# Idle matmuls from a VectorE-filled tile, and another order of the first groups, in a graph layer with a layer norm

## The reference, cut to what matters

```python
msg = jax.nn.relu(node_feat[src] + edge_attr)                      # a gather of 25000 rows
agg = jax.ops.segment_sum(msg, dst, num_segments=node_feat.shape[0])
h = node_feat + agg
h = jax.nn.relu(h @ W1 + b1) @ W2 + b2                             # 128 -> 256 -> 128
out = _layernorm(x + jax.nn.relu(h), axis=-1)
```

## Time and profile before

| | |
|---|---|
| median of three runs | 459.33 us (459.14 to 460.5) |
| profiled execution | 459.34 us |
| its span | 457.7 us |
| TensorE (PE) busy | 450.5 us, 98% |
| VectorE (DVE) busy | 433.3 us, 95% |
| ScalarE (ACT) busy | 394.6 us, 86% |
| GpSimd (POOL) busy | 370.1 us, 81% |
| mean granted TensorE clock | 0.997 |

### The profile page before, as it was taken

One profiled execution on the slowest core, in us unless ns is written; L12 is line 12 of the kernel. 1 busy time (PEld: TensorE's weight loads), 2 busy tenths in 40 slices (PEclk: granted clock), 3 DMA queues, 4 the chain that ended last, 5 costly groups with the idle time before them and its releaser, 6 DMA issues.

```text
span 457.7 us, 10675 instructions
## 1 busy us (share of the span) xinstructions
PE 450.5 (98%) x3046; PEld 380.4 (83%) x3046; DVE 433.3 (95%) x1759; ACT 394.6 (86%) x930; POOL 370.1 (81%) x403
## 2 busy tenths in 40 slices
PE   8999999999999999999999999999999999999995
PEld 7888888888888888888888888888888888888884
DVE  6899999999999999999999999999999999999996
ACT  3599888888888889988888888888888888888886
POOL 7778888888888878778888888888888888888842
PEclk9999999999999999999999999999999999999998
DMA  5576666666566666666666666666666666666632
GB/s 135 164 234 199 201 187 201 194 195 203 181 197 202 181 199 202 185 192 200 197 205 190 201 190 195 194 194 200 198 195 197 186 199 202 185 203 191 196 126 90
DMA packets 83870, 86.82 MB, mean 190 GB/s; under 512 B 12023, under 2 KB 79508, under 8 KB 83812
## 3 DMA queue, kind: packets, MB, share of 16 engines
q1 hardware_dynamic: 75044, 68.77, 48.2%
q0 software_dynamic: 8496, 17.38, 14.1%
q10 hardware_dynamic: 272, 0.00, 0.0%
HBM read 60.51 MB, written 25.60 MB: 188 GB/s over the span
## 4 chain that ended last, share of the span: by engine, by line
PE 98%; DVE 1%; ACT 0%; POOL 0%; issue 0%; DVEq 0%; POOLq 0%
PE h_ps L1052 38%; PE h1T_ps L1044 36%; PE hT_ps L965 11%; PE hT_ps L960 9%; PE h1T_ps L464 1%; PE prep_ps L451 0%; DVE stats L696 0%; PE hT_ps L936 0%; PE hT_ps L953 0%; DVE z L689 0%; PE h1T_ps L1032 0%; ACT std L851 0%; PE hT_ps L454 0%; ACT h1T L846 0%; PE h1T_ps L1025 0%
## 5 line engine op out<-in xcount | busy, mean ns | idle before, releaser
L135 POOL DMA_INDIRECT x_src<-in_x_dram,src_of x254 | 270.3, 1064 | 65.5 <-issue 59.8
L1052 PE MATMUL h_ps<-w_sb,h1T 128*128 128x128 f32 x1564 | 197.5, 276 | 0.0
L1044 PE MATMUL h1T_ps<-hT,w_sb 128*128 128x384 f32 x520 | 188.5, 485 | 0.0
L1052 PEld LDWEIGHTS h_ps<-w_sb,h1T 128*128 128x128 f32 x1564 | 185.2, 192 | 0.0
L846 ACT ACTIVATE h1T<-h1T_ps,b_sb 128x384 f32<-128x384 f32 (+1 forms) x262 | 151.5, 579 | 35.4 <-PE h1T_ps L1044 27.1
L1044 PEld LDWEIGHTS h1T_ps<-hT,w_sb 128*128 128x128 f32 x520 | 88.7, 191 | 34.2
L865 ACT ACTIVATE y<-z,shift,rstd 128x128 f32<-128x128 f32 x263 | 114.6, 483 | 1.1 <-DVE shift L716 0.2
L596 POOL TENSOR_SCALAR y<-z,rstd,shift 128x128 f32<-128x128 f32 x123 | 87.7, 713 | 13.5 <-DVE shift L716 9.0
L965 PE MATMUL hT_ps<-sel,msg_hi 128*128 128x216 f32 x250 | 94.8, 447 | 0.0
L696 DVE BATCH_NORM_STATS2 stats<-z 128x6 f32<-128x128 f32 x391 | 88.6, 282 | 0.1
L960 PE MATMUL hT_ps<-ident,x_sb 128*128 128x128 f32 x375 | 87.5, 272 | 0.0
(11 more groups left out here) (139 smaller groups left out, 187.9 us busy)
## 6 DMA issues: line engine op xcount, KB each, us to landing
x_sb<-in_x_dram SPq DMA_DIRECT2D x130, 192.0 KB, 2.4
out_dram<-y SPq DMA_DIRECT2D x130, 192.0 KB, 2.4
pre_msg<-in_edge_attr_dram SPq DMA_DIRECT2D x130, 128.0 KB, 2.8
x_src<-in_x_dram,src_of POOLq DMA_INDIRECT x254, 3.0
w_sb<-in_w_dram SPq DMA_DIRECT2D x2, 128.0 KB, 2.6
dst_rows<-in_dst_dram SPq DMA_DIRECT2D x1, 97.7 KB
x_src<-in_x_dram,first_pairs POOLq DMA_INDIRECT x6, 2.8
b_sb<-in_b_dram SPq DMA_DIRECT2D x1, 64.0 KB, 3.3
```

The lines of the kernel that those rows point to most:

```text
L135: nc.gpsimd.indirect_dma_start(out=c["x_src"][:, g % EB, k, :], out_offset=None, in_=x, in_offset=bass.IndirectOffsetOnAxis(ap=index, axis ...
L1044: nc.tensor.matmul(h1T_ps[h][:, 0:n, 0:p], w1_sb[:, h * 128:(h + 1) * 128], hT[:, 0:n, 0:p], start=True, stop=True).then_inc(h1_summed, 1)
L1052: last = nc.tensor.matmul(h2_ps[g % 2][0:p, t, :], h1T[:, h, t, 0:p], w2_sb[:, h, :], start=(h == 0 and t == 0 and not biased(g, c)), stop ...
```

## The change

The idle matmuls read a new tile `filler`, which VectorE fills with ones as its second instruction, and wait for that; there are nine of them instead of seven. The wait for the identity moves behind the two first search products. Group 0's six transposes (three into `hT_ps`, three into `rest_ps`) and the third search product stand together ahead of the wait for group 0's messages. `hidden_part` moves ahead of `turn_starts` and `sum_whole`. The product of group 0 by W2 is split and moves up: its first half stands ahead of the last product of group 1, its second half behind it, and both ahead of `turn_windows`. VectorE counts the first row ahead of the first addition and forms `msg_lo` ahead of `first_edges`. ScalarE copies the first part ahead of `whole_part`, takes `hidden(0, 0)` ahead of the fourth chunk's relu, and `copy_hT(1)` ahead of `source_nodes`. The loops over the later groups are the same.

```diff
--- before.py
+++ after.py
@@ -196,6 +196,7 @@
     sums_ps = prep_ps[0][0:1, R:R + FLAGS]
 
     ones_col = sb("ones_col", [128, 1])
+    filler = sb("filler", [128, 128])
     row_of = sb("row_of", [ROWS, 1])
     lowest = sb("lowest", [ROWS, 1])
     highest = sb("highest", [ROWS, 1])
@@ -233,6 +234,7 @@
     w1_loaded, w2_loaded = c["w1_loaded"], c["w2_loaded"]
     pool_consts = c["pool_consts"]
     ident_ready = sem("ident_ready")
+    filler_ready = sem("filler_ready")
     vec = sem("vec")
     eps_ready = sem("eps_ready")
     dst_f_ready = sem("dst_f_ready")
@@ -394,6 +396,7 @@
 
     def prepare_vector(dve):
         nc.vector.memset(dst_next[:, :], 0).then_inc(next_cleared, 1)
+        nc.vector.memset(filler[:, :], 1.0).then_inc(filler_ready, 1)
         nc.vector.memset(eps_col[:, :], LN_EPS).then_inc(eps_ready, 1)
         nc.vector.memset(ones_col[:, :], 1.0)
         nc.vector.memset(c["ones_row"][:, :], 1.0).then_inc(c["ones_row_ready"], 1)
@@ -442,17 +445,20 @@
 
     def prepare_tensor(pe):
 
-        pe.wait_ge(ident_ready, 1)
-        keep_busy(7)
+        pe.wait_ge(filler_ready, 1)
+        keep_busy(9)
         pe.wait_ge(dst_f_ready, 1)
         pe.wait_ge(row_of_ready, 1)
         pe.wait_ge(row_holds_ready, 1)
         for k in range(K):
             nc.tensor.matmul(found_ps[k], row_holds[:, k, :], dst_rows_f[:, 0:ROW + 1], start=True, stop=True).then_inc(row_found, 1)
+        pe.wait_ge(ident_ready, 1)
         pe.wait_ge(c["x_loaded"][0], 16)
-        for t in range(T):
-            nc.tensor.matmul(c["hT_ps"][:, t, :], c["x_sb"][:, 0, t, :], ident[:, :], is_transpose=True,
-                             start=(t == 0), stop=False, skip_group_check=True)
+        for ps in (c["hT_ps"], c["h2_ps"][1]):
+            for t in range(T):
+                nc.tensor.matmul(ps[:, t, :], c["x_sb"][:, 0, t, :], ident[:, :], is_transpose=True,
+                                 start=(t == 0), stop=False, skip_group_check=True)
+        find_ends(pe)
 
     def find_ends(pe):
 
@@ -461,7 +467,7 @@
     def keep_busy(times):
 
         for _ in range(times):
-            nc.tensor.matmul(c["h1T_ps"][0][:, 0, :], ident[:, :], ident[:, :], start=True, stop=True)
+            nc.tensor.matmul(c["h1T_ps"][0][:, 0, :], filler[:, :], filler[:, :], start=True, stop=True)
 
     def turn_starts(pe):
 
@@ -469,7 +475,7 @@
         nc.tensor.matmul(starts_ps, window_start[:, 0:1], ident[0:R, 0:R], start=True, stop=True).then_inc(starts_summed, 1)
 
     return dict(sync=prepare_sync, gpsimd=prepare_gpsimd, vector=prepare_vector, scalar=prepare_scalar, tensor=prepare_tensor,
-                find_ends=find_ends, turn_starts=turn_starts, count_start=count_start, first_edges=first_edges,
+                turn_starts=turn_starts, count_start=count_start, first_edges=first_edges,
                 split_edges=split_edges, start_edges=start_edges, check_ends=check_ends,
                 find_order=find_order, check_order=check_order, check_limits=check_limits, find_targets=find_targets,
                 check_targets=check_targets, set_general=set_general, sum_flags=sum_flags)
@@ -723,11 +729,11 @@
             return nc.vector.tensor_scalar(y[0:p, g % YB, t, :], z[0:p, g % ZB, t, :], rstd[0:p, g % SB, t:t + 1],
                                            shift[0:p, g % SB, t:t + 1], ALU.mult, ALU.add)
 
+        checks["count_start"](dve, 0)
         add_edge_attr(0, 0)
-        checks["count_start"](dve, 0)
         checks["count_start"](dve, 1)
+        low_part(0, 0)
         checks["first_edges"](dve)
-        low_part(0, 0)
         checks["split_edges"](dve)
         add_edge_attr(0, 1)
         checks["start_edges"](dve)
@@ -866,19 +872,19 @@
                                         bias=shift[0:p, g % SB, t:t + 1], scale=rstd[0:p, g % SB, t:t + 1])
 
         high_part(0, 0)
+        copy_part()
         whole_part(0, 1)
-        copy_part()
         high_part(0, 1)
         copy_rest()
         high_part(1, 0)
         act.wait_ge(c["starts_summed"], 1)
         nc.scalar.activation(c["starts_row"][:, :, 0:1].rearrange("a g k -> a (g k)"), c["prep_ps"][0][0:1, 0:R],
                              ACT.Copy).then_inc(c["starts_row_ready"], 1)
+        hidden(0, 0)
         high_part(1, 1)
-        hidden(0, 0)
         hidden(0, 1)
+        copy_hT(1)
         source_nodes()
-        copy_hT(1)
         high_part(2, 0)
         hidden(1, 0)
         high_part(2, 1)
@@ -1000,11 +1006,7 @@
             pe.wait_ge(c["first_sel_ready"], 1)
             pe.wait_ge(msg_hi_ready, 1)
             add(hT_ps, 0, FIRST_PART, msg_hi)
-            for t in range(T):
-                nc.tensor.matmul(rest_ps[:, t, :], x_sb[:, 0, t, :], ident[:, :], is_transpose=True,
-                                 start=(t == 0), stop=False, skip_group_check=True)
             add(rest_ps, FIRST_PART, 128, msg_hi)
-            checks["find_ends"](pe)
             pe.wait_ge(msg_lo_ready, 1)
             add(hT_ps, 0, FIRST_PART, msg_lo).then_inc(part_summed, 1)
             add(rest_ps, FIRST_PART, 128, msg_lo)
@@ -1055,20 +1057,20 @@
                 last.then_inc(h2_summed, 1)
 
         sum_first_parts()
+        pe.wait_ge(c["w1_loaded"], 16 * (1 + HC))
+        hidden_part()
         checks["turn_starts"](pe)
         sum_whole(1)
-        pe.wait_ge(c["w1_loaded"], 16 * (1 + HC))
-        hidden_part()
         turn_x(1)
         hidden_rest()
         sum_first(2)
         sum_first(3)
+        pe.wait_ge(c["w2_loaded"], 16)
+        output_sum(0, 0)
         sum_first(4, final=True)
+        output_sum(0, 1)
         pe.wait_ge(c["starts_row_ready"], 1)
         turn_windows(nc, pe, src_ps, dst_ps, c)
-        pe.wait_ge(c["w2_loaded"], 16)
-        output_sum(0, 0)
-        output_sum(0, 1)
         hidden_sum(1)
         turn_x(2)
         for i in range(5, 8):
```

## The result

| | median of the runs | lowest to highest | profiled execution | its span |
|---|---|---|---|---|
| before | 459.41 us (8 runs) | 459.14 to 460.50 | 459.34 | 457.7 |
| after | 461.16 us (8 runs) | 460.88 to 461.41 | 460.91 | 459.3 |

The ratio is 1.0035, with a 95% interval of 1.0026 to 1.0045: slower by some 1.7 us, where the forecast was 0.5. The time lies just above the predicted range.

A forecast was written before the change was run, and what follows sets the result against it. TensorE, busy 98% of the span, was taken as the bound, so only the start could change. Start 0, own work 0 and group 3's messages 0.55 us late gave 459.34 + 0.55 = 459.9 us; range 459.0 to 461.0 (own range 459.4 to 460.5).

The forecast's parts named there:

- The filler: Start of TensorE: idle passes begin at 1.08 instead of 2.17 us, direct gain 0, possibly an earlier clock rise.
- The two new waits: TensorE idles 0.56 us ahead of hidden_part and 0.37 ahead of hidden_rest, which eats the earlier clock.
- The window's chain: Window turned at 13.47 instead of 12.10, src_of at 13.96, 1.37 later, group 3's gathers issued at 14.64 and 15.91.
- VectorE's own lateness: Group 2's additions on VectorE come 0.37 us late, covered by the 0.55 of group 3's addition.
- The loop: From 24 to 440 us TensorE is always busy; the change leaves this as it is, with the same spacing.
- the landing of group 3's second gather: Issued at 15.91, it takes 2.9 us and lands at 18.8, making group 3's addition 0.55 us late.
- The first rival: Wait of group 3's addition for its second gather: the window's 1.37 us lateness arrives in full, 461.0 us; chance 0.15.
- TensorE itself: TensorE's own work reaches group 3's products at 19.76 against 19.73, on time, and then waits for messages.
- my 6.9: TensorE's clock rises at 6.9 us, if it stays 5.8 us behind the first idle pass.
- the bound of 4.6: Earliest clock rise considered, at 4.6 us, with the search itself running at 2.4 GHz.
- the second rival: Start of TensorE: an early clock rise is worth more than the order costs, 458.7 us; chance 0.15.
- the third: Rival: clock rises late, at 7.9 to 8.4, six transposes run slow, 1.0 us lost, 460.3 us; chance 0.12.

The follow-up runs named there:

- e6: After with group 3's two gathers taking source nodes of edges 0 to 255, so that they need no turned window: 459.92 us, ratio 1.0003.
- e15: After with six instead of nine idle matmuls, 14 16-column passes behind them and 8 ahead of layer one's first part: 460.84 us, ratio 1.0027.
- e2: Before with only the W2 passes moved ahead of turn_windows and copy_hT(1) ahead of source_nodes(): 461.12 us, ratio 1.0035.
- e1: After with the window turned ahead of the W2 passes again and source_nodes() ahead of copy_hT(1): 459.99 us, ratio 1.0012.
- e12: e7 with group 2's loads issued ahead of SyncE's wait for the window, plus 14 one-column memsets on VectorE: 460.16 us, ratio 1.0013 against before.
- e4: After with eight idle matmuls of 16 columns added ahead of hidden_part: 460.88 us, ratio 1.0028.
- e16: As e15, but with 12 instead of 14 passes of 16 columns at the start: 460.73 us, ratio 1.0021.
- e7: After with turn_starts and sum_whole(1) ahead of hidden_part, group 1's last product ahead of W2, the window between W2's halves: 459.90 us, ratio 1.0003.
- e18: e7's order with the small TensorE passes of e15, but 10 instead of 14 at the start: 461.02 us, ratio 1.0029.
- e9: After with 14 one-column memsets added to VectorE's program in a wait: 460.67 us, ratio 1.0023.
- e17: e7's order with the small TensorE passes of e16, 12 at the start: 460.90 us, ratio 1.0027.

## Why the prediction was wrong

What held:

- *The filler.* First idle pass at 1.10 (forecast 1.08), and no direct gain.
- *The two new waits.* `hidden_part` waits for ScalarE's copy, `hidden_rest` for the second, 8.28 and 10.40 against a forecast of 8.74 and 10.60.
- *The window's chain.* The window was turned (L179) at 13.43 (forecast 13.47), `src_of` at 13.87 (13.96), gathers at 14.54 and 15.81 (14.64, 15.91).
- *VectorE's own lateness*, 0.37 in the forecast: 0.34 in e6, where it waited for no gather.
- *The loop*: its spacing is unchanged, and TensorE never waits in it.

What failed above all is one term, the landing of group 3's second gather: "Issued at 15.91, the gather moves its data in the quiet stretch", and from it "I take 2.9, near the lower end because of the quiet stretch: 18.8". It landed at 19.73, 3.92 us from issue. The stretch was quiet (0.29 busy), but a share over 16 engines doesn't tell whether one of them is held, and a transfer in 16 parts lands with its last. What was held was one part, by TensorE's instruction fetch: fifteen parts had landed by 18.57, 2.76 us from issue, close to the 2.9 that I had taken. That the fetch does it is shown by the landing that follows its end in thirteen traces, by the sixteenth packet, which starts in after as the fetch ends, and by e15, which moved the fetch by program and moved the late part with it, from the gather to `x_sb`. What it cost can be estimated: from the landing to the first product after takes 1.57 us (19.73 to 21.30), so a landing at 18.57 would have given 20.14, and TensorE itself was free at 20.18. That is 0.45 us late instead of 1.57, so the held part is worth about 1.1 us, and without it the messages would have been 0.41 late where the forecast had 0.55. No run shows after without a held part. That fetch and part share one DMA engine is inferred: the records don't name engines.

The first rival is what happened: it was to decide "where the landing takes over 3.4 us", and e2, e1 and e6 confirm its place and price. Its time came true, its mechanism (a gather that takes as long wherever it stands) did not: the place of the fetch decides. I gave it 0.15, reading the row of before (3.7 us) as contention with other loads. In before too the last part stood alone (18.16 against 17.66), and that was to be seen in its landings; one of its packets starts at 16.91, just as VectorE's fetch (16.60 to 16.91) ends.

A smaller term failed too: "TensorE itself ... 19.76. It is on time". It was free at 20.18 in after, 0.45 late, hidden behind the wait for the messages. 0.32 of that is a wait for `x_sb` of group 2 until 15.69. SyncE issued that load at 12.50 instead of 12.28, for the window landed late (SyncE went on at 12.08 instead of 11.86), and one part of it was late as well: fifteen landed by 15.08, the last at 15.64. No fetch ran then, so a part can also be late from another cause, which stays open. I had let the window's landing stand as fixed; over the twenty traces it lies between 11.84 and 13.58 us (13.58 in e12).

The clock rose at 4.29 us, below my 6.9 and beyond the bound of 4.6, and was still worth almost nothing: TensorE then waited for `msg_hi` until 7.21 and for the copy until 8.28, and reached the window within 0.04 us of the forecast. So the second rival's mechanism was there without its gain, and the third's (transposes hold the clock down) did not come: in after the clock had risen before the six transposes (5.87 to 6.5), and fell at none of them. What the Trainium skill says of transposes (TensorE: Matmul & The Clock Gate, "Part 4: PE-mode transpose") stays untested here for a clock that is still low.

Open: what sets the time of TensorE's fetch. 32 instructions more than in after (e4) left it at 17.36, 76 more (e15) moved it by 2.4 us, 68 more (e16) by 0.6; 60 more than in e7 (e18) moved it by 2.1.

## What to carry to other kernels

A transfer that lies on the critical chain lands with the last of its parts: read its landings part by part and look for an instruction fetch of the same moment before you call a stretch quiet. Work that is exchanged on the busy engine at no cost to it can still delay the start of a chain over three other engines, and what that chain can bear is its slack against the worst landing, not the usual one. An experiment that pads a program moves its fetches too, so look where they fell before reading its time.

## What the runs showed of the hardware that was not expected

- An instruction fetch of 16 KB is one packet; the first of each trace lasts 0.92 to 1.54 us. In before they come 15.8 to 21.4 us apart (the first at 17.13, 38.52 and 54.34). VectorE's first one is 8 KB and takes 0.3 to 0.7 us. One of 16 parts of the transfer that is moving then can land up to 2.0 us behind the others (15.10 and 17.12 for `x_sb` in e15).
- TensorE's clock rose at 7.99 us in before, 4.29 in after and between 4.3 and 10.3 in the experiments; from 4.26 (e9) to 6.68 (e1) in kernels whose idle passes at the start are those of after. It came late where passes of 16 columns stood in the place of passes of 128 in e16 (7.21) and e18 (10.3), but not in e15 (4.68) and e17 (4.85), which have the same kind of passes. No rule is drawn from that.
- Fourteen one-column memsets on VectorE cost 0.22 us together.
